# Three of a scan's products moved from VectorE to GpSimd, and a rounding pass moved from GpSimd to ScalarE

## What is computed

```python
delta = softplus(einsum('er,brl->bel', dt_proj_w, dt_lo) + dt_proj_b)
dA = exp(d_t[..., None] * A)
state = state * dA + (d_t * u_t)[..., None] * B_t[:, None, :]
y_t = einsum('ben,bn->be', state, C_t)
...
y = (y + D * u) * silu(z)
x = x + y
x = x + moe(layernorm(x))
```

## Time and profile before

| quantity | value |
|---|---|
| timed executions | 301.12, 302.5, 307.67 us, median 302.5 us |
| the profiled execution's own time | 300.18 us |
| its span | 298.4 us |
| mean granted TensorE clock | 0.878 of full speed |
| busy: PE, DVE, ACT, POOL | 252.1, 219.0, 175.5, 220.4 us |

### The profile page before, as it was taken

One profiled execution on the slowest core, in us unless ns is written; L12 is line 12 of the kernel. 1 busy time (PEld: TensorE's weight loads), 2 busy tenths in 40 slices (PEclk: granted clock), 3 DMA queues, 4 the chain that ended last, 5 costly groups with the idle time before them and its releaser, 6 DMA issues.

```text
span 298.4 us, 4932 instructions
## 1 busy us (share of the span) xinstructions
PE 252.1 (84%) x1508; PEld 223.5 (75%) x1508; DVE 219.0 (73%) x381; ACT 175.5 (59%) x384; POOL 220.4 (74%) x180
## 2 busy tenths in 40 slices
PE   8959777857867587894979999999999999999950
PEld 7748555546745475683967999999999999999940
DVE  3899998999999999999652556667584848484610
ACT  2798766967995775577052566364747465564410
POOL 1799599869959999999716836868585868777552
PEclk9996997897979855576687999999999999999995
DMA  6579610080005431051161354563636464644111
GB/s 166 212 248 313 228 64 0 5 315 1 0 1 196 162 114 64 35 176 37 63 226 59 82 208 178 174 210 136 220 117 209 137 214 159 219 173 175 34 46 36
DMA packets 15073, 40.38 MB, mean 135 GB/s; under 512 B 2922, under 2 KB 9900, under 8 KB 12112
## 3 DMA queue, kind: packets, MB, share of 16 engines
q1 hardware_dynamic: 11792, 33.15, 33.0%
q0 software_dynamic: 2816, 6.32, 6.1%
q10 hardware_dynamic: 448, 0.70, 0.9%
HBM read 32.72 MB, written 8.49 MB: 138 GB/s over the span
## 4 chain that ended last, share of the span: by engine, by line
PE 47%; POOL 5%; DVE 5%; issue 4%; DMA 2%; POOLq 1%; ACT 0%; SPq 0%
PE ps L983 13%; PE ps L985 13%; PE ps L984 13%; DVE h L1186 3%; POOL expert_rows L387 2%; PE ps L992 2%; PE ps L1001 2%; DVE hc L1197 1%; PE ps L1074 1%; POOL dbu L342 1%; POOL w1lo L417 1%; PE ps L966 1%; DMA xe<-expert_rows 1%; DMA expert_rows<-xrow,sloti 1%; PE ps L810 1%
## 5 line engine op out<-in xcount | busy, mean ns | idle before, releaser
L1186 DVE TENSOR_TENSOR_SCAN h<-ps,dbu 128x512 f32<-128x512 f32 x64 | 74.6, 1207 | 2.0 <-ACT ps L536 1.9
L342 POOL TENSOR_TENSOR dbu<-du,bsb 128x1024 f32<-128x1024 f32 x31 | 72.7, 2364 | 0.7 <-DMA bsb<-b_rows 0.4
L536 ACT ACTIVATE ps<-delta,anegs 128x255 f32<-128x255 f32 x128 | 53.3, 462 | 9.5 <-DVE h L1186 6.9
L1358 DVE SCALAR_TENSOR_TENSOR htlo<-ps,hthi 128x320 fp32r<-128x320 f32 x64 | 30.4, 487 | 35.0 <-ACT hthi L690 35.0
L429 POOL TENSOR_TENSOR w2lo<-w2raw,w2hi 128x512 fp32r<-128x512 f32 x30 | 38.3, 1305 | 12.0 <-ACT w2hi L681 11.9
L791 PE MATMUL ps<-stack,sels 64*128 64x256 f32 x64 | 19.3, 390 | 32.2 <-DVE hc L1197 29.0
L810 PE MATMUL ps<-cst,hc 128*128 128x128 f32 x256 | 46.4, 341 | 0.0
L791 PEld LDWEIGHTS ps<-stack,sels 64*128 64x128 f32 x64 | 12.3, 238 | 41.5 <-issue 41.4
L810 PEld LDWEIGHTS ps<-cst,hc 128*128 128x128 f32 x256 | 37.6, 176 | 4.5 <-issue 2.2
L983 PE MATMUL ps<-xthi,w1hi 128*128 (+1 forms) x128 | 40.5, 317 | 0.0
L983 PE MATMUL ps<-hthi,w2hi 128*128 128x320 f32 x128 | 40.3, 315 | 0.0
(11 more groups left out here) (154 smaller groups left out, 465.1 us busy)
## 6 DMA issues: line engine op xcount, KB each, us to landing
w1raw<-in_w SPq DMA_DIRECT2D x8, 1024.0 KB, 4.8
w2raw<-in_w SPq DMA_DIRECT2D x8, 1024.0 KB, 4.9
bsb<-b_rows SPq DMA_DIRECT2D x7, 1024.0 KB, 7.2
expert_rows<-fill SPq DMA_DIRECT2D x1, 2580.0 KB, 15.9
xe<-expert_rows SPq DMA_DIRECT2D x8, 258.0 KB, 5.5
out<-x SPq DMA_DIRECT2D x4, 256.0 KB, 5.2
xnat<-in_x SPq DMA_DIRECT2D x1, 768.0 KB, 7.3
xe<-expert_rows SPq DMA_DIRECT2D x8, 64.5 KB, 5.6
```

Source lines behind the costliest of these rows:

```text
L342: nc.gpsimd.tensor_tensor(dbu[j % DRING][:], du[:, :, None, cols(b)].to_broadcast([P, EC, 2, L]), bsb[b % 2][:, None, 2 * p:2 * p + 2, :]. ...
L536: ins = nc.scalar.activation(decays(g % SLOTS_DA)[:, c, i * L + 1:(i + 1) * L], delta[:, c, b * L + 1:(b + 1) * L], ACT.Exp, scale=anegs[: ...
L1186: nc.vector.tensor_tensor_scan(h[g % HRING][:, c].rearrange("p n t -> p (n t)"), decays(g % SLOTS_DA)[:, c, :], dbu[g % DRING][:, c].rearr ...
L1358: nc.vector.scalar_tensor_tensor(out=htlo[:, f, :], in0=ps[:, f % 4, 0:CAP], scalar=0.0, in1=hthi[:, f, :].bitcast(F32), op0=ALU.max, op1= ...
```

## The change

Four things are edited. (1) The products of steps 6, 14 and 22 (`POOLED`) are made by GpSimd (`pooled`), from the states and from `csb`, an SBUF copy of the C bank; GpSimd makes product 6 between drives 10 and 11, product 14 between drives 18 and 19, product 22 between drives 26 and 27. (2) ScalarE makes that copy, behind the decay of step g + 2. (3) The rounding part of softplus for batches 1 to 3, one instruction of GpSimd, becomes two copies of ScalarE with a bias (`round_off`), ahead of the logarithm. (4) The waits follow: the scan of step 9, 17 or 25 and the sum of step 6, 14 or 22 wait for GpSimd's product, the C broadcast of step 7, 15 or 23 for ScalarE's copy, and the counts of VectorE's products are lowered (`made_by_dve`).

```diff
+POOLED = [PAIRS * b + 6 for b in range(B - 1)]
+def made_by_dve(g):
+    return g + 1 - sum(1 for n in POOLED if n <= g)
...
+        csb = sm("csb", [P, 2 * L])
...
-            def softplus_d(b):
-                pool.wait_ge(s["sp_exp"], b + 1)
-                nc.gpsimd.tensor_scalar(spd, spe, 1.0, -1.0, ALU.add, ALU.add).then_inc(s["sp_d"], 1)
...
+            def pooled(k):
+                g = POOLED[k]
+                pool.wait_ge(s["scan_done"], SLOTS_DA + g + 1)
+                pool.wait_ge(s["csb_done"], k + 1)
+                pool.wait_ge(s["ysum_done"], g - SUMS + 1)
+                nc.gpsimd.tensor_tensor(hc[g % SUMS][:].rearrange("p c n t -> p c (n t)"),
+                                        h[g % HRING][:].rearrange("p c n t -> p c (n t)"),
+                                        csb[:, None, :].to_broadcast([P, EC, 2 * L]), ALU.mult
+                                        ).then_inc(s["pooled_done"], 1)
             for j in range(1, STEPS):
                 b, p = divmod(j - DRING, PAIRS)
+                if p == PAIRS - 1 and 0 <= b < B - 1:
+                    pooled(b)
...
                     if p == 3:
-                        softplus_d(b + 1)
                         softplus_w(b + 1)
...
+            def round_off(b):
+                nc.scalar.activation(spd, spe, ACT.Copy, bias=1.0).then_inc(s["sp_s"], 1)
+                act.wait_ge(s["sp_s"], b)
+                nc.scalar.activation(spd, spd, ACT.Copy, bias=-1.0).then_inc(s["sp_d"], 1)
             def logs(b):
                 act.wait_ge(s["sp_exp"], b + 1)
+                if b:
+                    round_off(b)
                 nc.scalar.activation(spl, spe, ACT.Ln, bias=1.0).then_inc(s["sp_ln"], 1)
...
                 if g + 2 < STEPS:
                     decay(g + 2)
+                if g in POOLED:
+                    act.wait_ge(s["c_psum"], g + 1)
+                    k = POOLED.index(g)
+                    if k:
+                        act.wait_ge(s["pooled_done"], k)
+                    nc.scalar.activation(csb[:], ps[:, CBANK, :], ACT.Copy).then_inc(s["csb_done"], 1)
...
+                elif g - 1 in POOLED:
+                    pe.wait_ge(s["csb_done"], POOLED.index(g - 1) + 1)
                 elif g:
-                    pe.wait_ge(s["mult_done"], g)
+                    pe.wait_ge(s["mult_done"], made_by_dve(g - 1))
...
             def add_state(g, tiles):
-                pe.wait_ge(s["mult_done"], g + 1)
+                if g in POOLED:
+                    pe.wait_ge(s["pooled_done"], POOLED.index(g) + 1)
+                else:
+                    pe.wait_ge(s["mult_done"], made_by_dve(g))
...
-                if g >= HRING:
-                    dve.wait_ge(s["mult_done"], g - HRING + 1)
+                if g - HRING in POOLED:
+                    dve.wait_ge(s["pooled_done"], POOLED.index(g - HRING) + 1)
+                elif g >= HRING:
+                    dve.wait_ge(s["mult_done"], made_by_dve(g - HRING))
...
-                mult(g)
+                if g not in POOLED:
+                    mult(g)
```

More of the change, by code:

```diff
@@ L205, in build @@
             "xp_psum hi_done brow_done brow_out b_lo_in b_hi_in stack_done v_psum "
-            "sp_abs sp_relu sp_exp sp_ln sp_d sp_t sp_w delta_done du_done a_exp a_neg "
+            "sp_abs sp_relu sp_exp sp_ln sp_s sp_d sp_t sp_w delta_done du_done a_exp a_neg "
             "z_stats z_var z_rstd z_mean z_scale zs_done zt_psum zt_done wg_psum wg_done "
-            "b_psum b_done c_psum da_done half_done scan_done dbu_done first_dbu mult_done ysum_done "
+            "b_psum b_done c_psum da_done half_done scan_done dbu_done first_dbu mult_done pooled_done csb_done ysum_done "
             "gate_done x1_done ln_var ln_eps ln_rstd ln_neg ln_scale xn_done xt_psum xt_done lg_psum top_bias top_exp "
```

## The result

Four executions of the changed kernel took 309.73 to 314.45 us, median 313.32; four of the kernel before took 301.12 to 307.67, median 302.77. The ratio is 1.0348, 95% interval 1.0299 to 1.0396: 10.55 us more by the medians, where 10.5 had been forecast on 301.3. Every ratio in this document compares executions within 1.5% of the fastest of their kernel, which leaves out one here of either kernel and three, three, one and six of the twelve of experiments 8 to 11; the medians and ranges given count all of them.

What follows compares the result with a forecast made beforehand. The prediction took VectorE, busy 96.37 of 100 us in the scan with GpSimd close behind, as the bound. Its terms 5.3 + 1.3 + 3.9 = 10.5 us, added to 301.3, gave 311.8 us, range 304.5 to 317.

Steps and rivals of the forecast that it cites:

- What bounds, and GpSimd late at step 6: VectorE bounds the scan; GpSimd's product 6 ends at 55.5, so the scan of step 9 starts 3.1 us late.
- Step 6, +5.3: Gate of batch 0 at 61.15 instead of 55.84, behind GpSimd's late product and TensorE's chain at half clock: +5.3 us.
- Step 14, +1.3: Gate of batch 1 at 89.65 against 88.25, GpSimd being ready: +1.3 us taken, +0.85 at full clock.
- the four pieces at half clock: TensorE's sum of step 14 and the three pieces behind it, from 84.15, take 5.4 us at half clock.
- +0.8 for ScalarE's copy: At step 14 ScalarE's copy of C delays the table load and decay, so the scan of step 17 starts 0.8 us later.
- Step 22, +3.9: Scan of step 25 2.6 us late, then TensorE at half clock: gate at 124.25 against 120.38, +3.9 us.
- The sum, 10.5: The delays at steps 6, 14 and 22 add up to 10.5 us, all of which reaches the end.
- The rounding and the copies: ScalarE's two rounding copies, 1.3 us in all, and its copy of C at step 6, 1.5 us with the wait, are hidden.
- The price of the product, 2.36 us: GpSimd's product takes 2.36 us, like a drive of the same shape; bounds 1.19 and 3.5 us.
- the third rival: Port: product and scan exclude each other, each product making one scan longer, 3 x 2.3 us more: 318.7 us; chance 0.06.
- The second rival: Not slower: GpSimd is early enough at steps 6, 14 and 22: 302 us, at best 297.9; chance 0.12.
- the first (clock stays up): TensorE's clock stays up and only GpSimd's lateness counts: 3.1 + 0.85 + 2.6 = 6.5 us, so 307.8; chance 0.14.

Runs made afterwards that it cites:

- experiments 8 to 11: Against the kernel before, GpSimd makes products 8, 16 (0.9947); 8, 16, 24 (0.9981); 9, 17 (0.9987); 8, 16 with the rounding back on GpSimd (0.9979).
- experiment 3: The changed kernel with each of GpSimd's three products one drive earlier in its queue; 307.29 us, ratio 1.0187 against the kernel before.
- experiment 6: The changed kernel with 36 idle matmuls on TensorE ahead of the sum of step 6; 309.65 us, ratio 1.0282 against the kernel before.
- experiment 1: The changed kernel with only the rounding moved to ScalarE and no product moved; 302.63 us against 301.29 for the kernel before, ratio 1.0032.
- experiment 2: The changed kernel with the three products still on GpSimd but the rounding back on GpSimd; 315.13 us, ratio 1.0447 against the kernel before.
- experiment 9: The changed kernel with GpSimd making the products of steps 8, 16 and 24 instead, ahead of its addition of x; 302.40 us, ratio 0.9981 against the kernel before.
- experiment 8: The changed kernel with GpSimd making only the products of steps 8 and 16, ahead of its addition of x; 300.91 us against 301.68 before, ratio 0.9947.
- experiment 4: The changed kernel with four buffers for the states instead of three; 311.43 us, ratio 1.0335 against the kernel before.
- experiment 7: The changed kernel with only the product of step 14 on GpSimd, rounding still on ScalarE; 302.0 us against 301.42 for the kernel before, ratio 1.0028.

## Why the prediction was right

**What bounds, and GpSimd late at step 6: right.** The scan of step 9 started 12.59 us behind the product of step 5 instead of 9.55, 3.04 us late (3.1 forecast), with GpSimd's product as its releaser. The product that left bought nothing, as said.

**Step 6, +5.3: mechanism right, size 0.9 too large.** The chain on TensorE was taken at half clock throughout, 5.4 us. It was half for the first three pieces; then the granted clock rose, and the sum of step 7 took 1.15 us instead of 1.97, so the chain took 4.63. The wait therefore showed at the product of step 8 (1.26 us) and not at the gate. In experiment 3 the clock stayed at half to the end, and the 0.69 us in front of the gate stood as forecast. Experiment 6 splits the 4.4 us: 3.1 GpSimd's lateness, 1.3 the clock.

**Step 14, +1.3: the step in it that failed is the four pieces at half clock.** They ran at full clock (1.09). (The prediction's own times, 89.65 against 88.25, would give +1.4.) The forecast +0.8 for ScalarE's copy was there, 0.76 us. The other 1.48 us stand elsewhere: the product of step 13 waited 2.10 us instead of 0.62, because TensorE's eight convolution matmuls at 77.51 took 3.60 us instead of 2.31. In the kernel before, TensorE's and VectorE's rows are

```profile
71.29 2.31 PE L757 MATMUL ps<-ctxs,cwb 128*128 128x256 f32 x8
...
74.91 1.22 DVE L1197 TENSOR_TENSOR hc<-h,ps 128x1024 f32<-128x1024 f32 x1 [0.62 <-DVE h L1186]
```

I don't count this as shown to come from the change: the same piece took 1.88 to 3.60 us over the profiles compared, among them 3.44 in experiment 1, which moves no product (there it began 1 us earlier against the scan, and cost 0.13). But waits as long as this one (2.22 us in experiment 2, 2.03 in 9) came only in kernels with a moved product, so a part may be the change's; that stays open.

**Step 22, +3.9: right, 0.4 too large.** The scan of step 25 came 2.21 us late against the gate of batch 1 (2.6 forecast), since GpSimd was 2.36 us earlier than before instead of 2.0. TensorE's 1.97, 0.79 and 1.97 us at half clock added 1.29 (1.3 forecast).

**The sum, 10.5: closer than its terms, by luck.** The three terms were off by -0.9, +0.9 and -0.4 us, and the first two cancel; without the 1.48 us that may not be the change's, the three stretches give 8.7. The interval of the ratio, 3.0% to 4.0%, is itself 3 us wide. The time of 313.32 is 1.5 above the 311.8 forecast, since the executions of the kernel before came out at 302.77 and not at the 301.3 taken.

**The rounding and the copies: right.** Hidden, by experiment 1 and by the 1.03 us that ScalarE still waited at 50.36.

**The price of the product, 2.36 us: right**, 2335 to 2349 ns. That speaks against the third rival too. In the changed kernel the products of steps 6 and 22 ran while VectorE waited, but that of step 14 (2.33 us from 87.59) ran beside a scan, which took its usual 2.34 us from 88.27; in experiment 8 that of step 8 took 2.37 us beside a scan of 2.33. The Trainium skill (Perfetto Trace Analysis, "Optimizing Scalar/DVE Operations") warns that moving work between VectorE and GpSimd might not help because they share an SBUF read port; the trace shows no such price for these operands: the product takes no longer than a drive, and the 64 scan instructions took 1208 ns on average, 1207 before. It agrees with the narrower rule of the Trainium skill (SBUF — State Buffer, "Who interferes with whom"), by which a VectorE instruction with at most one SBUF input, outside its two-port modes, does not contend with GpSimd: VectorE's scan and product read one operand each from PSUM. The second rival (GpSimd early enough) holds at step 14 alone, the first (clock stays up) there too.

## What to carry to other kernels

Before work goes to a less busy engine, look at what that engine does at the moment the result is wanted, and not at its share of the span: the same 2.34 us of GpSimd cost 4.4 us at step 6 and 1.0 at step 14, and at steps 8 and 16, inside GpSimd's own wait, they made a kernel 0.5% faster, though not in every execution. Then list everything behind the instruction that will wait, on every in-order queue: a deeper ring alone gave nothing here (experiment 4), because TensorE's queue held back the next broadcast just as long. A starved TensorE may also come back at half clock, and that is part of the price.

## What the runs showed of the hardware that I had not expected

- Keeping TensorE at work for 8.30 us left the clock at full even after 1.08 us without work (experiment 6); after 9.29 us without work it was granted 0.50 for the next 3.2 us, and after 2.31 us eight transposes took 1.09 us, which is full. The length of the last wait alone does not say which: eight transposes took 1.97 us after 5.30 us without work in experiment 7, and also after 1.75 us in experiment 9.
- After the long wait the clock came back while only short pieces ran: in the changed kernel ahead of the sum of step 7 (1.15 us), in experiment 3 not yet (1.97 us), with the same instructions.
- A float32 matmul of 128x128 shows as two records in the trace: 36 of them as 72 records in 8.30 us.
